# Four-layer graph network: constant products woven into the last merge, weights of layers 2 and 3 loaded earlier, count scatters redistributed

## The reference, cut to what matters

```
h_all = einsum('nd,ted->nte', h, W) + b      # layer 2, one of 5 steps
a = segment_sum(h_all[src, etypes], dst)
h = gru_cell(a, h, w_ih, w_hh, b_ih, b_hh)
```

## Time and profile before

| | us |
|---|---|
| median of 3 runs (8886.32 to 8889.57) | 8888.87 |
| the profiled execution's own time | 8891.25 |
| its span, first to last instruction | 8890.0 |
| mean granted clock of TensorE, share of full | 0.767 |

### The profile page before, as it was taken

The page is one execution under the profiler, slowest core; times in us unless marked ns, Lnnn a source line. Parts: engine busy times, 40 slices in busy tenths (PEclk is TensorE's granted clock), DMA queues, the critical chain, the costliest instruction groups (busy, mean ns, idle before and its releaser), DMA issues. The chain is left out here.

```text
span 8890.0 us, 111137 instructions
## 1 busy us (share of the span) xinstructions
PE 5328.1 (60%) x39647; PEld 4855.0 (55%) x39647; DVE 4045.6 (46%) x8424; ACT 2223.2 (25%) x5853; POOL 5594.2 (63%) x5805
## 2 busy tenths in 40 slices
PE   4545624545466667344455677676889999933323
PEld 3333424445366666344444666676679999923323
DVE  7666524443444444566664445454422222233333
ACT  0000013333133332233322444444111111021221
POOL 7777677777777777777777777777510000057776
PEclk8777667777588886677776888888689999966665
DMA  7665252222244441343333555555178888821111
GB/s 240 207 198 180 47 54 62 63 62 57 53 115 116 114 116 41 108 120 113 116 80 105 151 152 152 151 152 151 24 292 325 329 329 326 331 77 27 27 27 27
DMA packets 440766, 1203.87 MB, mean 135 GB/s; under 512 B 161729, under 2 KB 235330, under 8 KB 399570
## 3 DMA queue, kind: packets, MB, share of 16 engines
q1 hardware_dynamic: 203188, 707.03, 22.8%
q0 software_dynamic: 237024, 489.72, 22.5%
HBM read 1072.84 MB, written 120.95 MB: 134 GB/s over the span
## 5 line engine op out<-in xcount | busy, mean ns | idle before, releaser
L1264 PE MATMUL ps<-pool 128*106 128x128 f32 (+2 forms) x19344 | 2571.4, 301 | 5.3 <-DVE pool L1164 5.3
L1264 PEld LDWEIGHTS ps<-pool 128*106 128x106 f32 (+2 forms) x19344 | 2547.9, 185 | 8.4 <-DVE pool L1164 5.6
L1222 ACT ACTIVATE ACC<-ps 72x256 f32 (+1 forms) x2418 | 1010.4, 418 | 1990.4 <-PE ps L1264 1745.9
L482 POOL DMA_INDIRECT ACC<-t,ACC x416 | 392.5, 944 | 1490.2 <-DVE ps L1793 1363.7
L1243 PE MATMUL ps<-ident,pool 128*128 128x128 f32 (+1 forms) x204 | 90.7, 445 | 1882.3 <-DVE pool L1122 1882.3
L1243 PEld LDWEIGHTS ps<-ident,pool 128*128 128x128 f32 (+1 forms) x204 | 36.9, 181 | 1921.1 <-issue 1921.1
L764 POOL DMA_INDIRECT cnt_d<-pool x806 | 833.3, 1034 | 320.7 <-issue 234.3
L1122 DVE COPY pool<-pool 128x128 f32<-128x128 f32 (+1 forms) x204 | 46.8, 229 | 1967.7 <-DMA pool<-d_h,srcT_s 663.1
L1291 POOL DMA_INDIRECT pool<-a_h,srcT_s x806 | 776.1, 963 | 245.5 <-issue 244.9
L1164 DVE TENSOR_TENSOR pool<-pool,ps 128x1024 f32<-128x1024 f32 (+1 forms) x807 | 928.3, 1213 | 0.0
L1291 POOL DMA_INDIRECT pool<-d_h,srcT_s x806 | 772.2, 958 | 245.6 <-issue 198.0
(11 more groups left out here) (300 smaller groups left out, 6601.2 us busy)
## 6 DMA issues: line engine op xcount, KB each, us to landing
ACC<-cnt_d SPq DMA_DIRECT2D x172, 1600.0 KB, 8.7
pool<-cnt_d SPq DMA_DIRECT2D x88, 1600.0 KB, 8.7
cnt_d<-pool SPq DMA_DIRECT2D x26, 3200.0 KB
ACC<-key_d SPq DMA_DIRECT2D x31, 1792.0 KB
ACC<-key_d SPq DMA_DIRECT2D x25, 2048.0 KB, 8.1
pool<-seg_d SPq DMA_DIRECT2D x100, 129.0 KB
cnt_d<-pool POOLq DMA_INDIRECT x806
pool<-a_h,srcT_s POOLq DMA_INDIRECT x806
```

The costliest lines, as they stand in the source:

```text
L482: g.indirect_dma_start(out=gb[b][:, k, :], out_offset=None, in_=table, in_offset=bass.IndirectOffsetOnAxis(ap=idx[:, c:c + 1], axis=0)).th ...
L1222: a.activation(win[:, 0:NPL, bass.ds(reg, 128)], pl[0].rearrange("p (i c) -> p i c", c=128), ACT.Copy).then_inc(*(tile_out if last else A) ...
L1264: mm = t.matmul(o, gbr[:, tile % RT, M * i:M * i + M], oh, start=True, stop=True)
```

## The change

1. **Wide products of constants on PE, in pass d only** (`tensor_idle`): each multiplies 128 x 128 bf16 values (the identity's bits) by 512 bf16 columns of `sel[16]` into PSUM bank 7, which nothing reads afterwards. 40 of them stand ahead of the wait for the shares; 2 behind each scale product of the first two chunks (10 products, so 20); 2 behind each block's products (31 blocks, so 62).
2. **Count scatters in pass d**: 344 instead of 345 between the gathers, 18 instead of 48 behind the wait for the last tile, two instead of one behind each merged block (62 instead of 31), 32 at the end as before.
3. **Layer 2's preparation moved**: SP issues the 12 loads of layer 2 and the 2 of layer 3 right behind the shares; DVE zeroes `wnn` ahead of its slot work and adds the biases in the merge's fifth round, behind a wait for the 12 loads; GpSimd, not DVE, sets the row of ones, behind a wait for the shares. The index list is built in step 0 of layer 2, after the first eight table rows. The first barrier stays, the loads of edge weights and types stay behind it.

```diff
+        BESIDE_D, MERGED_D = 18, 2 * NS
+        GAP_D = TAIL_ + BESIDE_D + MERGED_D + AFTER
-            p0, p1 = EARLY + GAP * layer, NT - GAP - LATE
+            p0, p1 = EARLY + GAP * layer, NT - GAP_D - LATE
@@ gpsimd_pass
-                scatter_counts(s0 + TAIL_, s0 + TAIL_ + BESIDE)
+                scatter_counts(s0 + TAIL_, s0 + TAIL_ + (BESIDE if layer < 3 else BESIDE_D))
@@ gpsimd_merge
-                s0 = (p0 if layer < 3 else p1) + TAIL_ + BESIDE
+                s0, each = (p0 + TAIL_ + BESIDE, 1) if layer < 3 else (p1 + TAIL_ + BESIDE_D, 2)
+                if layer == 3:
+                    g.wait_ge(share_out.sem, sh0 + 48)
+                    g.memset(xT[D:D + 1, :], 1.0).then_inc(*const.one())
                 for b in range(NS):
                     g.wait_ge(slot_mm.sem, smm0 + b + 1)
-                    scatter_counts(s0 + b, s0 + b + 1)
-                scatter_counts(s0 + NS, s0 + NS + AFTER if layer < 3 else NT)
+                    scatter_counts(s0 + each * b, s0 + each * (b + 1))
+                s0 += each * NS
+                scatter_counts(s0, s0 + AFTER if layer < 3 else NT)
@@ sync_slots, behind the three writes of the shares
                 if following is not None:
                     sync_weights(*following)
+                else:
+                    sync_l2_weights()
@@ vector_slots, ahead of vector_wholes()
+                if layer == 3:
+                    vector_l2_zeros()
+            def tensor_idle(count):
+                if layer == 3:
+                    for _ in range(count):
+                        t.matmul(ps[7][:, 0:512], ident.bitcast(BF16)[:, 0:128], sel[16].bitcast(BF16), start=True, stop=True)
@@ vector_merge, end of round j
+                    if layer == 3 and j == 4:
+                        vector_l2_biases()
@@ tensor_scales, behind each scale product
+                        tensor_idle(2 if j < 2 else 0)
@@ tensor_merge_slots
             def tensor_merge_slots():
+                tensor_idle(40)
                 t.wait_ge(share_out.sem, sh0 + 48)
...
                         if b:
                             tensor_node(b - 1)
+                        tensor_idle(2)
                 tensor_node(NS - 1)
+        def vector_l2_zeros():
+            v.memset(wnn, 0.0).then_inc(*V.one())
+            mark["wnn"] = V.now()
+        def vector_l2_biases():
+            v.wait_ge(*w2.now())
+            v.tensor_tensor(out=brz, in0=bih[:, 0:2], in1=bhh[:, 0:2], op=ALU.add).then_inc(*V.one())
+        def sync_l2_weights():
+            s.wait_ge(*mark["wnn"])
+            s.dma_start(wc[0:D, :], I["L2_W"][:, :]).then_inc(*w2.one())
...
+            for p0 in (0, D):
+                s.dma_start(w3[p0:p0 + D, :], I["L3_W"][:, :]).then_inc(*w3_in.one())
@@ after pass d's norm_and_transpose() and barrier()
+        t.wait_ge(*const.now())
+        t.wait_ge(*w2.now())
@@ the old preparation
-        vector_l2_zeros()
-        sync_l2_prep()
-        for p0 in (0, D):
-            s.dma_start(w3[p0:p0 + D, :], I["L3_W"][:, :]).then_inc(*w3_in.one())
-        vector_l2_prep()
         barrier()
@@ vector_step, step 0
                 vector_rows(0, 0, AHEAD)
+                vector_l3_lists()
```

More of the change, by code:

```diff
@@ L1600, in batchnorm @@
             barrier()
+        w2, w3_in = dsig("w2_in"), dsig("w3_in")
+        wc, wzr, wnn = wl[0:D + 1, 0:256], wl[:, 256:384], wl[:, 384:512]
+        bih, bhh, brz = wl[:, 512:515], wl[:, 515:518], wl[:, 518:520]
+        w3 = wl[:, 520:1544]
+        def vector_l2_zeros():
[7 more added lines that the diff above has]
+            s.dma_start(wc[0:D, :], I["L2_W"][:, :]).then_inc(*w2.one())
+            s.dma_start(wc[D:D + 1, :], I["L2_gnn_b"].rearrange("t e -> (t e)").unsqueeze(0)).then_inc(*w2.one())
+            for p0, x in ((0, "L2_wih"), (D, "L2_whh")):
+                s.dma_start(wzr[p0:p0 + D, 0:D], I[x][:, D:2 * D]).then_inc(*w2.one())
+                s.dma_start(wzr[p0:p0 + D, D:2 * D], I[x][:, 0:D]).then_inc(*w2.one())
+                s.dma_start(wnn[p0:p0 + D, p0:p0 + D], I[x][:, 2 * D:3 * D]).then_inc(*w2.one())
+                s.dma_start(bih[p0:p0 + D, :], I["L2_bih"][:, :]).then_inc(*w2.one())
+                s.dma_start(bhh[p0:p0 + D, :], I["L2_bhh"][:, :]).then_inc(*w2.one())
+            for p0 in (0, D):
+                s.dma_start(w3[p0:p0 + D, :], I["L3_W"][:, :]).then_inc(*w3_in.one())
         gat("a", 64, 16, None, (128, 32, I[L + "We2"], I[L + "as_e2"], I[L + "ad_e2"]),
@@ L1613, in build @@
         barrier()
-        idx_in, w2 = dsig("idx_in"), dsig("w2_in")
+        t.wait_ge(*const.now())
+        t.wait_ge(*w2.now())
+        idx_in = dsig("idx_in")
         for dst_, src_ in ((ew, "ewT"), (idx16, "et16T")):
             s.dma_start(dst_, I[src_][:, :]).then_inc(*idx_in.one())
[L1619 to L1624, removed]
+        both = acc4[:, 0, :]
         r_, z_, n_ = (gates[:, 512 * j:512 * (j + 1)] for j in range(3))
@@ L1642, in build, with vector_l3_lists @@
         half_mm, y_sum, merge_mm, win_add = sig("half_mm"), sig("slot_sum"), sig("merge_mm"), sig("window_add")
[L1644 to L1659, removed]
+        def vector_l3_lists():
             v.wait_ge(*idx_in.now())
```

## The result

The changed kernel takes 8923.28 us (median of 6 runs, 8920.96 to 8927.64) against 8887.6 for the kernel before beside it: ratio 1.0043, interval 1.0032 to 1.0053. It is slower, by 0.4%. The forecast was 8855; the rival "the clock is lost or never comes" had said 8931.

What follows compares the result with a forecast made beforehand. GpSimd's chain of count scatters was taken to bound the start of layer 2; the last scatter going out 34.2 us earlier gave 8857 profiled, 8855 for the median. The 8-in-10 range was 8846 to 8888.

Steps and rivals of the forecast that it cites:

- the clock is lost or never comes: Rival for the merge: wide and lone scale products paid at low clock, together +42.5 us, 8931; chance 0.14.
- The clock in the merge: PE enters the merge at 1.00 and stays there: blocks 1.91 us instead of 2.95, merge 85.0 us.
- The entry: Ahead of the merge: 40 wide products take 17.1 us at low clock or about 12 if it rises; taken as 0.
- The stay: Inside the merge: the clock holds at 1.00, argued from 40 dense products ahead and no pause of PE.
- the 2.7 at the start: Rival's term at the merge's start: 40 wide products end 2.7 us too late if the clock never rises.
- Start of the merge: First scale product at 6311.3 instead of 6312.00: scatter -1.3, memset +0.2, 14 loads +0.4 (0 to +4).
- Memset of ones: GpSimd sets the row of ones while waiting before the first block's node product; bounded by 1 and 10 us.
- The pause of 3.9: Among the last 32 scatters: moves with the 14 loads into GpSimd's wait, costing nothing; kept, it is +3.9.
- Preparation: Ahead of layer 2: 14.0 us leave the other path, 32 us ahead of the counts; gives nothing by itself.
- Scatters: GpSimd in the merge: 10.2 us per round against PE's 9.6, never waits; last scatter at 6451.8, gain 34.2 us.
- Scale products alone or side by side: First ten scale products stand one by one: 1.84 us alone at low clock, 2 x 0.46 at full.
- The conditional sum: With the clock held: blocks' own work 1.47 us, last scatter at 6451.8, gain 34.2 us.

Runs made afterwards that it cites:

- e1: The changed kernel with 64 instead of 40 wide products ahead of the merge; ratio 1.0049 to the kernel before.
- e2: The changed kernel with 64 wide products ahead of the merge and none inside it; ratio 1.0001 to the kernel before.
- e6: The changed kernel with 64 wide products ahead, none behind scale products, eight behind each block; ratio 1.0013 to the kernel before.
- e7: The changed kernel with 64 wide products ahead, eight behind every scale product, none behind blocks; ratio 1.0042 to the kernel before.
- e9: The changed kernel with 64 wide products ahead, six behind each chunk's third and fifth scale product, none behind blocks; ratio 0.9973 to the kernel before.
- e13: e2 with the 64 wide products of its lead cut to 8 rows, on a slower chip; ratio 0.9989 to the kernel before.
- e14: e9 with only the wide products inside the merge cut to 8 rows, on a slower chip; ratio 1.0009 to the kernel before.
- e11: The changed kernel with 64 wide products ahead, four behind every scale product, none behind blocks; ratio 1.0114 to the kernel before.
- e5: The changed kernel with 64 wide products ahead, eight behind every scale product and every block; ratio 1.0094 to the kernel before.
- e8: The changed kernel without wide products, its scatters moved to where GpSimd was idle; ratio 0.9962 to the kernel before.
- e4: The kernel before plus only the change's wide products, scatters and preparation as before; ratio 1.0042 to the kernel before.
- e3: The changed kernel with all wide products deleted; ratio 1.0001 to the kernel before.
- e16: e8 without GpSimd's wait for merged blocks in pass d, plus the wide products of e9; ratio 0.9946 to the kernel before.
- e10: The changed kernel with 64 wide products ahead, eight behind scale products of the first two chunks only, none behind blocks; ratio 1.0018 to the kernel before.

## Why the prediction was wrong

*The step that failed is "The clock in the merge"*: "If PE enters the merge at 1.00 and stays there". From it came blocks of 1.91 us and a merge of 85.0 us; the merge ran at 0.50 throughout, with blocks of 3.61 us, and took 165.2 us. Two errors lie in the step.

The entry: "40 take 17.1 us if the clock never rises ... and about 12 if it rises after some 6 us, in time. I take 0; nothing else waits for PE there". The clock rose sooner (1.00 from 6297 on, the lead having begun at 6294.32) and the 40 took 9.7 us. PE then stood for 3.70 us, and in the kernel after that pause is where the clock fell. I asked only whether the lead would be late. This error cost nothing that can be told: e1 has no pause and is at 1.0049, the kernel after at 1.0043.

The stay decides: "Against: 40 dense products ahead and no pause of PE inside the merge" was no argument. e1 and e2 entered at 1.00 without a pause and lost it within the first scale products; e6, e7 and e9 show that the scale products are what lets it fall. That this is for their 8 rows of 128 is likely by e13 and e14, and not shown. The hint was there, a full PE row at 0.50 over 79 us, and I read it only as "uninterrupted work is not enough for a rise", not as a question of which products make up that work. In the first chunks, where the change did put two wide products behind each scale product, it fell with two (e1), later with four (e11), not with eight (e5, e7), and with six behind every second or third it came back after each dip (e9).

The prices of the rival "the clock is lost or never comes" came near: it had +42.5, the profiled span grew by 36.1. Blocks cost 3.61 where it had 2.95 + 0.85 = 3.80, the two wide ones taking 0.83 as priced and the block's five products 2.16 from start to start instead of 2.33; the first ten scale products cost 2.93 each with their wide ones where it had 2.69. The merge grew by 41.6 where its terms for it make 26.5 + 16.6 = 43.1, and the 2.7 at the start did not come, the lead being early. The last scatter came 38.4 us later. Part of the rest is luck: pass d ended about 4.3 us sooner where one scatter is 1.3. Its last gather already went out 4.4 us sooner (6246.18 against 6250.60), ahead of the 30 scatters that were taken away behind it, and from run to run that gather moves by more than this, as said above.

The other steps, one by one:

- *Start of the merge*: the shares' issue to the first scale product took 8.69 us against 8.66 before; 14 loads cost nothing, inside the bound of 0 to +4.
- *Memset of ones*: 2.76 us on GpSimd, hidden in its wait, as taken.
- *The pause of 3.9* did not move away with the loads: 3.00 us are left ahead of 6504.48, 2.7 more than the usual 0.30, so 1.2 of 3.9 was gained. I had tied it to the wrong thing: in all 18 profiles it stands ahead of the 114th scatter behind pass d's last gather, in e8 at 6416.75, some 26 us before SP issues the loads of edge weights and types. It is 4.22 and 4.42 us in the two kernels that issue the 14 loads there (before and e4), 2.99 to 3.35 in the others. What it is, no run shows.
- *Preparation*: gone, worth nothing by itself (e3: 1.0001). The other path was far ahead of the counts, as said (PE idle 28.57 us before the first count product; 32 forecast).
- *Scatters*: "GpSimd is the later of the two and never waits" hung on the clock; in the kernel after it waited 92.0 us for node products (54.6 before).
- *Scale products alone or side by side*: one by one, as said, and dearer than priced: 2.03 us alone where it had 1.84, and at full clock 1.10 where it had 2 x 0.46 = 0.92. Three side by side take 1.11 at full clock.
- *The conditional sum*: with the clock held (e9) blocks took 1.62 (0.15 above the 1.47 forecast), the last scatter went out 5.3 us later than forecast and the gain was 24 instead of 34.

A choice ahead of these was wrong too. I took it as given that GpSimd follows the blocks and asked how to make blocks faster. The wait at each block was the order's, not the data's: filling GpSimd's idle time (0.38%, e8) and then taking the wait away gained 0.55% at half clock, twice the 0.27% that the held clock gave, and left the clock nothing to give that could be measured (e16).

## What to carry to other kernels

Before paying work to hold TensorE's clock, look at which products make up the stretch, not at how full the PE row is: here bare products of 8 rows lost a clock of 1.00 within 5 us (e2, e6), and did so with no pause of PE too (e10, and e1 with two wide ones behind each). Filler of 128 rows between those very products held it, filler of 8 rows did not, and filler that was too thin was dearer than none, since it ran at 0.50 itself (e1, e11). Put filler between groups that run side by side on different rows, not inside one, where it ends the overlap (e9 against e7). And when the chain that ends last runs through an engine that waits for another, ask first whether the wait is the data's or the order's.

## What the runs showed that I had not expected

- Products 8 rows deep, back to back for 27 us (e13), left the clock at 0.50; the same products at 128 rows had it at 1.00 before the lead ended (kernel after, e1, e2, e14).
- What kept the clock did not raise it: the merge's block and node products left it at 0.50 in the last 15 us of the merge before, and kept it at 1.00 in the last 10 us of e7's.
- A scale product alone takes as long as three side by side: 2.03 us against 2.05 at 0.50, 1.10 against 1.11 at 1.00.
